# Two rounds of routed experts: setup of the routing tables rearranged in `experts`

## The chip, the cores and the metric

The kernel runs on one core of a Trainium2 chip. The metric is the device time in microseconds of one execution; the figure of a version is the median of its runs. Engines are named as in the profile: PE is TensorE, DVE is VectorE, ACT is ScalarE, POOL is GpSimd, and SP is the engine whose queue issues most transfers.

## The reference

The input has 4096 tokens of 256 features. Four layers are added to it one after the other; the change touches the two that route tokens to experts.

```python
# layer 1: eight experts, two per token, chosen from the context
logits = einsum('bsd,de->bse', context, Wg) + bg
scores, idx = top_k(logits, 2);  weights = softmax(scores)
combine = sum(one_hot(idx, E) * weights[..., None], axis=-2)
h = relu(einsum('bsd,edf->bsef', layernorm(x), W1) + b1)
x = x + einsum('bsed,bse->bsd', einsum('bsef,efd->bsed', h, W2) + b2, combine)
# layer 2: eight experts, one per token, chosen from the normalised x,
# at most tokens / 8 per expert, gate value softmax(logits) of the chosen one
...
# layer 3: attention with 16 heads; layer 4: gated FFN with fake quantisation
```

## The kernel before

`two_layers` calls `experts` twice, then `attention` and `gated_ffn`. In the first call (`choices` 2, `gate_source` the context, `capacity` None, 40 tiles of 256 slots) each token goes to two experts; in the second (`choices` 1, no gate source, a fixed capacity, 16 tiles) to one. The names of both calls' tiles begin with top_ in the trace, since it drops digits.

Each call has a setup and a loop over expert tiles. In the setup, the token rows (x_all, 32 tiles of 128 rows, loaded in four quarters) are measured for the layer norm on DVE (L649 to L654); ACT takes the root (L587 in the first call, behind the last `logits_copy`; L577 in the second), and DVE refines it and makes the scale and shift. PE transposes the gate source in groups of four tiles, multiplies by the gate weights and transposes the logits back (L424, L433, L440), with ACT copying in between (`gate_copy`, `logits_copy`). DVE then makes the choices: best logit, one-hot mask, lowest index, and PE counts how many tokens of each expert come before a token (L454, L455). From this DVE works out the slot of each token, as tile number and lane. The inverse, which token sits in a slot, comes from matrix products: for each choice DVE writes the masks pick_lane (128 x 4096, f16) and pick_tile (128 x 2560 in the first call, 128 x 1024 in the second), and PE multiplies them, 32 matmuls per choice (L461). From the product DVE makes row_of_slot, the row numbers for the gathers (L780 to L784). Before it waits for the product it writes expert_of_tile, which names the expert of a tile (L772 to L776).

Meanwhile ACT normalises x_all in place (L582; in the second call DVE does it, L668), and SP stores the result and the weights of each token by expert (by_token, eight columns in the same rows) to the DRAM tensor normed. `softmax_of_two` makes these weights on DVE between the picks of the two choices. POOL gathers rows of normed by row_of_slot (`gather`, L348), 128 rows at a time and two gathers to a tile. Six tiles are gathered ahead. Then, per tile, PE transposes the rows (L476), ACT and DVE split them into two f16 parts, PE does the first layer (L493 to L495), ACT the bias and the relu (L615), DVE splits (L805, L807), PE does the second layer (L511 to L513), DVE adds b2 and scales (`result`), and POOL adds the rows to x_sum in DRAM by an indirect transfer. Expert weights are loaded by SP into four buffers (`load_expert`), 512 KB each; ACT writes the high f16 part (`split_hi`) and DVE the low one (`split_lo`, L638), which also frees the buffer for the next expert's load. Expert 0 is split in the setup, the others one at a time before the tiles 1 to 7.

The order on each engine is the order in the code. `order(...)` makes the engine wait until the instruction has written; `order.tick` only counts it. SP's queue is, in order: gate weights and biases, context (first call), x, the copy of x to x_sum (first call), b2, expert 0, then a wait on s_normed, the normalised rows (4 MB in one transfer and two of 128 KB), a wait on s_wts, the token weights (128 KB in pieces of 32 bytes, and two of 4 KB), and then, in a loop, experts 1 to 7. POOL waits for the row table, s_stored and s_wstored ahead of its first gather. [...]

## Time and profile before

| what | value |
|---|---|
| median of three runs | 1664.61 us (1660.75 to 1664.78) |
| profiled execution | 1662.72 us, its span 1661.0 us |
| busy share of the span | PE 79%, PEld 64%, DVE 72%, ACT 50%, POOL 29% |
| first call, setup to the first expert product | 0 to 98.9 us |
| first call, expert tiles | 98.9 to about 546 us |
| second call, setup | about 553.6 to 626.2 us |
| PE busy, granted clock 0 to 60 us | 28.3 us, 0.86 |
| PE busy, granted clock 60 to 86 us | 4.6 us, 0.50 |
| DVE busy 60 to 86 us | 25.0 us |
| PE busy, granted clock 190 to 540 us | 349.1 us, 1.00 |

All times are microseconds from the start of the span. Busy time of an engine leaves out its waits and the issue of transfers. In the rows below, "L" with a number is the line of the kernel, "xN" the number of instructions that a row holds (its duration is from the start of the first to the end of the last), and square brackets give the idle time of the engine ahead of the row and what ended it. A buffer called top_w_hi or top_w_lo can be any of the small tiles that live in the unused parts of the weight buffers.

### The profile page before, as it was taken

The numbers are of one execution on the slowest core, as the hardware profiler recorded it, in microseconds if no ns is written. First come the engines' busy times: TensorE is split into PE (matmuls) and PEld (weight loads), VectorE is DVE, ScalarE is ACT, GpSimd is POOL, SyncE is SP. The second block draws the span as 40 slices with busy tenths as digits, with TensorE's granted clock in tenths as the row PEclk, the third lists the DMA queues.
The fourth block names the chain that finished last, engine by engine and source line by source line (L and its number), as shares of the span: only waits on it lengthen the run. The fifth ranks groups of instructions, "written<-read, shape, count | busy, mean of one in ns | idle before, by whom it ended". The sixth has DMA issues, their size and how long they took to land. (4 is left out here: it accounts for less than half of the span.)

```text
span 1661.0 us, 31750 instructions
## 1 busy us (share of the span) xinstructions
PE 1311.1 (79%) x10558; PEld 1068.2 (64%) x10559; DVE 1196.2 (72%) x2040; ACT 830.6 (50%) x1240; POOL 481.7 (29%) x480
## 2 busy tenths in 40 slices
PE   6069999999999529999368999999998499760087
PEld 3059888888898208998346887778877344320076
DVE  3869756655665478965178888888888576998854
ACT  3546533333333226733046555555555466987654
POOL 0035755555542114553212222222224000000000
PEclk9579999999999769999769888888888599995599
DMA  9548432233321656832430000000000100336211
GB/s 326 172 150 244 106 49 45 48 51 51 47 47 23 191 162 178 232 53 34 97 98 10 11 9 9 9 9 9 9 10 1 39 1 0 140 127 240 101 45 58
DMA packets 104166, 134.71 MB, mean 81 GB/s; under 512 B 16529, under 2 KB 88209, under 8 KB 102289
## 3 DMA queue, kind: packets, MB, share of 16 engines
q1 hardware_dynamic: 82576, 103.73, 19.1%
q0 software_dynamic: 21504, 29.83, 10.8%
q8 instruction: 55, 0.90, 0.2%
q14 instruction: 31, 0.25, 0.0%
HBM read 88.43 MB, written 45.11 MB: 80 GB/s over the span
## 5 line engine op out<-in xcount | busy, mean ns | idle before, releaser
L615 ACT ACTIVATE top_x_all<-top_h_ps,top_b1T 128x256 f32<-128x256 f32 x448 | 185.7, 472 | 311.6 <-PE top_h_ps L495 311.6
L493 PE MATMUL top_h_ps<-top_xT_hi,top_w_hi 128*128 128x256 f16 x896 | 246.3, 275 | 0.0
L494 PE MATMUL top_h_ps<-top_xT_lo,top_w_hi 128*128 128x256 f16 x896 | 246.2, 275 | 0.0
L495 PE MATMUL top_h_ps<-top_xT_hi,top_w_lo 128*128 128x256 f16 x896 | 246.1, 275 | 0.0
L513 PE MATMUL top_y_ps<-top_w_hi,top_x_all 128*128 x896 | 244.2, 273 | 0.0
L511 PE MATMUL top_y_ps<-top_w_hi,top_x_all 128*128 x896 | 244.2, 273 | 0.0
L512 PE MATMUL top_y_ps<-top_w_lo,top_x_all 128*128 x896 | 244.2, 273 | 0.0
L805 DVE CAST top_x_all<-top_x_all 128x512 f16<-128x512 f32 x224 | 98.5, 440 | 145.7 <-ACT top_x_all L615 145.7
L807 DVE TENSOR_TENSOR top_x_all<-top_x_all 128x512 f16<-128x512 f32 x224 | 155.7, 695 | 7.7
L353 POOL DMA_INDIRECT x_sum<-top_x_all,top_row_of_slot x56 | 101.5, 1812 | 173.3 <-DVE top_x_all L819 120.0
L1129 PEld LDWEIGHTS attn_out_ps<-attn_v,attn_probT 128*128 128x128 f32 x1024 | 127.1, 199 | 4.4
L1615 PE MATMUL ffn_ps<-ffn_dT_hi,ffn_yT 128*128 128x256 f16 x192 | 53.8, 280 | 91.1 <-DVE ffn_yT L1895 91.1
L1129 PE MATMUL attn_out_ps<-attn_v,attn_probT 128*128 128x17 f32 x1024 | 125.4, 265 | 0.0
L1028 POOL TENSOR_TENSOR attn_q_parts<-attn_q,attn_q_parts 128x512 f16<-128x512 f32 x32 | 37.1, 1158 | 303.9 <-ACT attn_q_parts L1192 303.9
L1119 PE MATMUL attn_S<-attn_ident,attn_prob 128*128 128x128 f32 x512 | 94.2, 344 | 38.9 <-ACT attn_prob L1208 38.8
L353 POOL DMA_INDIRECT x_sum<-top_x_all,top_rows_out x56 | 91.6, 1636 | 109.7 <-DVE top_x_all L819 98.5
L1212 ACT ACTIVATE attn_probT<-attn_S 128x1024 f32<-128x1024 f32 x64 | 65.5, 1023 | 89.9 <-PE attn_S L1119 89.9
L1327 DVE COPY_PREDICATED attn_S<-attn_masked,attn_tiny 128x1024 f32<-128x1024 int32 x64 | 104.4, 1632 | 1.3 <-PE attn_S L1113 1.3
L1119 PEld LDWEIGHTS attn_S<-attn_ident,attn_prob 128*128 128x128 f32 x512 | 74.0, 174 | 48.1 <-ACT attn_prob L1208 44.9
L348 POOL DMA_INDIRECT top_xg<-normed,top_row_of_slot x56 | 60.0, 1072 | 149.9 <-DVE top_row_of_slot L784 133.3
L1583 PE MATMUL ffn_ps<-ffn_yT,ffn_guT_hi 128*128 128x512 f16 x192 | 74.0, 385 | 27.5 <-ACT ffn_u_all L1656 23.3
L494 PEld LDWEIGHTS top_h_ps<-top_xT_lo,top_w_hi 128*128 x896 | 88.4, 99 | 10.9
(299 smaller groups left out, 3219.4 us busy)
## 6 DMA issues: line engine op xcount, KB each, us to landing
top_staged<-in_L_xattn_W SPq DMA_DIRECT2D x32, 512.0 KB, 6.2
top_staged<-in_L_ffn_w SPq DMA_DIRECT2D x32, 512.0 KB, 5.4
up_raw<-ffn_u_all SPq DMA_DIRECT2D x48, 256.0 KB, 2.1
ffn_yT<-up_raw SPq DMA_DIRECT2D x12, 1024.0 KB, 4.7
normed<-top_x_all SPq DMA_DIRECT2D x2, 4096.0 KB, 14.1
top_w_lo<-in_ctx SPq DMA_DIRECT2D x4, 1024.0 KB, 9.9
top_x_all<-in_x SPq DMA_DIRECT2D x4, 1024.0 KB, 11.8
x_sum<-top_x_all SPq DMA_DIRECT2D x4, 1024.0 KB, 11.6
```

The source lines that it names most:

```text
L353: nc.gpsimd.indirect_dma_start(out=x_sum, out_offset=bass.IndirectOffsetOnAxis(ap=rows, axis=0), in_=y[p][:, k, :], in_offset=None, comput ...
L493: nc.tensor.matmul(out, hi, xT_hi[p][:, c, :], start=(c == 0), stop=False)
L494: nc.tensor.matmul(out, hi, xT_lo[p][:, c, :], start=False, stop=False)
L495: last = nc.tensor.matmul(out, lo, xT_hi[p][:, c, :], start=False, stop=(c == DC - 1))
L511: nc.tensor.matmul(out, h_hi[p][:, fc, rows], hi, start=(fc == 0 and k == 0), stop=False, skip_group_check=True)
L512: nc.tensor.matmul(out, h_hi[p][:, fc, rows], lo, start=False, stop=False, skip_group_check=True)
L513: last = nc.tensor.matmul(out, h_lo[p][:, fc, rows], hi, start=False, stop=(fc == FC - 1), skip_group_check=True)
L615: last = nc.scalar.activation(h32[:, fc * R:(fc + 1) * R], h_ps[:, b, q * R:(q + 1) * R], ACT.Relu, bias=b1T[:, bass.ds(e * FC + fc, 1)], ...
L807: V.tensor_tensor(lo, part, hi, ALU.subtract).then_inc(s_hl[p], 1)
L1119: mm = nc.tensor.transpose(S[:, r, c, :], prob[:, r * HC + c, :], ident[:])
L1129: mm = nc.tensor.matmul(out_ps[:, h * V1:(h + 1) * V1], probT[:, h, :], v32[i][:, 2 * c + r, :], start=True, stop=True)
L1327: V.copy_predicated(S[:, r], masked[:].unsqueeze(1).to_broadcast(wide), tiny[:].unsqueeze(1).to_broadcast(wide)).then_inc(s_mask[r][p], 1)
```

## The change

The same values are computed.

- In the first call ACT takes the root ahead of the last `logits_copy`, not behind it. The normalised rows are written to the context's buffer (n_all), not in place. The wait for the copy of x to x_sum moves behind the normalisation and the split of expert 0.
- The rows are normalised and stored in quarters, each with its own wait on SP; POOL waits for 96 on s_stored.
- The load of b2 moves on SP's queue from ahead of expert 0 to behind the stores of the token weights. DVE waits for it ahead of `split_lo(0)`, not ahead of the logits.
- Three pairs of DVE instructions in the routing of the first call, one in that of the second, become one `scalar_tensor_tensor` each.
- The three products and sums that make by_token in the first call move from DVE to POOL, ahead of its gathers.
- Each choice writes pick_tile first and pick_lane in four quarters, and PE starts its matmuls quarter by quarter.
- The expert table is written behind the row table, with a semaphore of its own (s_experts), for which PE and ACT wait.

```diff
+        n_all = gate_all
...
-            sp.dma_start(b2_all[:].rearrange("p e d -> p (e d)"), broadcast_rows(b2, P, E * D)).then_inc(s_b2, 16)
...
             load_expert(0)
-            sp.wait_ge(s_normed, 1)
-            sp.dma_start(n_tiles, x_all[:]).then_inc(s_stored, 16)
+            for q in range(4):
+                sp.wait_ge(s_normed, q + 1)
+                sp.dma_start(n_tiles[:, q * n:(q + 1) * n, :], n_all[:, q * n:(q + 1) * n, :]).then_inc(s_stored, 16)
...
+            sp.dma_start(b2_all[:].rearrange("p e d -> p (e d)"), broadcast_rows(b2, P, E * D)).then_inc(s_b2, 16)
             with sp.Fori(1, E) as e:
                 load_expert(e)
...
+            if choices == 2:
+                pool.wait_ge(s_share, 1)
+                order.tick(nc.gpsimd.tensor_tensor(by_token[:], onehot[0], weight[0][:].unsqueeze(2).to_broadcast([P, T, E]), ALU.mult))
+                order(nc.gpsimd.tensor_tensor(both, onehot[1], weight[1][:].unsqueeze(2).to_broadcast([P, T, E]), ALU.mult))
+                nc.gpsimd.tensor_tensor(by_token[:], by_token[:], both, ALU.add).then_inc(s_wts, 1)
             pool.wait_ge(s_table, 1)
-            pool.wait_ge(s_stored, 48)
+            pool.wait_ge(s_stored, 96)
...
-                pe.wait_ge(s_pick, c + 1)
                 for t in range(T):
+                    if t % (T // 4) == 0:
+                        pe.wait_ge(s_pick, 4 * c + t // (T // 4) + 1)
...
             transpose_in(0, 0)
+            pe.wait_ge(s_experts, 1)
...
-            logits_copy(GROUPS - 1)
             if gate_source is not None:
                 act.wait_ge(s_var, 1)
                 nc.scalar.activation(rstd[:], rtmp[:], ACT.Sqrt).then_inc(s_root, 1)
+            logits_copy(GROUPS - 1)
...
-            dve.wait_ge(s_b2, 16)
             dve.wait_ge(s_lt, GROUPS)
...
-                order(V.tensor_scalar(work, work, float(E), None, ALU.mult))
-                order(V.tensor_tensor(work, work, of_expert(expert_no[:]), ALU.add))
+                order(V.scalar_tensor_tensor(work, work, float(E), of_expert(expert_no[:]), ALU.mult, ALU.add))
...
-                    order(V.tensor_scalar(work, onehot[c], -3e38, None, ALU.mult))
-                    order(V.tensor_tensor(logits, logits, work, ALU.add))
+                    order(V.scalar_tensor_tensor(logits, onehot[c], -3e38, logits, ALU.mult, ALU.add))
...
-                order.tick(V.tensor_tensor(pick_lane[c], lanes(P), by_lane(slot_mod[c][:], P), ALU.is_equal))
                 order(V.tensor_tensor(pick_tile[c], lanes(NS), by_lane(slot_div[c][:], NS), ALU.is_equal))
-                V.tensor_tensor(pick_tile[c], pick_tile[c], by_lane(token_v[:], NS), ALU.mult).then_inc(s_pick, 1)
+                V.tensor_tensor(pick_tile[c], pick_tile[c], by_lane(token_v[:], NS), ALU.mult)
+                for q in range(4):
+                    part = slice(q * (T // 4), (q + 1) * (T // 4))
+                    V.tensor_tensor(pick_lane[c][:, part], lanes(P)[:, part], by_lane(slot_mod[c][:], P)[:, part],
+                                    ALU.is_equal).then_inc(s_pick, 1)
...
             V.tensor_copy(row_of_slot[:], row_f[:]).then_inc(s_table, 1)
+            order(V.tensor_scalar(expert_f[:], lane_no[:, 0:NT], start_of[:, 1:2], None, ALU.is_ge))
+            for e in range(2, E):
+                order(V.scalar_tensor_tensor(expert_f[:], lane_no[:, 0:NT], start_of[:, e:e + 1], expert_f[:],
+                                             ALU.is_ge, ALU.add))
+            V.tensor_copy(expert_of_tile[:], expert_f[:]).then_inc(s_experts, 1)
             dve.wait_ge(s_table, 1)
+            dve.wait_ge(s_experts, 1)
+            dve.wait_ge(s_b2, 16)
             split_lo(dve, 0)
```

## Rows read from the trace of the kernel before

**Rows 1.** Timeline of the first call, last logits to the routing: start, duration, engine, line.

```profile
38.99 0.59 ACT L569 ACTIVATE top_w_lo<-top_xT_ps 8x512 f32<-8x512 f32 x1 [2.31 <-PE top_xT_ps L433]
39.59 1.28 ACT L587 ACT_TABLE_LOAD   x1
39.63 0.41 PE L440 MATMUL top_y_ps<-top_ident,top_w_lo 8*128 8x8 f32 x4 [0.68 <-ACT top_w_lo L569]
...
41.15 0.35 DVE L656 RECIPROCAL top_rstd<-top_rstd 128x32 f32<-128x32 f32 x1 [6.29 <-ACT top_rstd L587]
...
44.73 0.42 DVE L685 TENSOR_TENSOR top_w_hi<-top_y_ps,top_bg_sb 128x256 f32<-128x256 f32 x1 [2.10 <-DMA top_b_all<-in_L_xattn_b]
...
46.10 0.29 DVE L696 TENSOR_SCALAR top_w_hi<-top_w_hi 128x256 f32<-128x256 f32 x1
```

**Rows 2.** Timeline of the first call, picks, shares, expert table, reading of the product.

```profile
60.02 4.42 DVE L768 TENSOR_TENSOR top_w_hi<-top_lane_no,top_slot_mod 128x4096 f16<-128x4096 f32 x1
...
69.96 0.17 DVE L758 TENSOR_SCALAR top_weight<-top_weight 128x32 f32<-128x32 f32 x1
...
70.78 0.42 DVE L761 TENSOR_TENSOR top_by_token<-top_w_hi,top_weight 128x256 f32<-128x256 f32 x1
...
82.11 2.31 PE L461 MATMUL top_h_ps<-top_w_hi 128*128 128x80 f16 x32 [9.70 <-DVE top_w_hi L770]
82.24 1.74 DVE L774 SCALAR_TENSOR_TENSOR top_expert_f<-top_lane_no,top_start_of,top_expert_f 128x40 f32<-128x40 f32 x6
...
84.53 0.24 DVE L780 TENSOR_SCALAR top_pad_f<-top_h_ps 128x80 f32<-128x80 f32 x1 [0.34 <-PE top_h_ps L461]
```

**Rows 3.** Timeline of the first call from the row table on; then line L348's summary.

```profile
85.87 4.63 DVE L638 SCALAR_TENSOR_TENSOR top_w_lo<-top_staged,top_w_hi 128x1024 f16<-128x1024 f32 x4
...
88.57 1.64 POOL L348 DMA_INDIRECT top_xg<-normed,top_row_of_slot  x1 [0.30 <-issue]
...
95.83 1.11 PE L476 MATMUL top_xT_ps<-top_ident,top_xg 128*128 128x128 f32 x4 [11.41 <-DMA top_xg<-normed,top_row_of_slot]
...
98.94 0.42 PE L493 MATMUL top_h_ps<-top_xT_hi,top_w_hi 128*128 128x256 f16 x1
...
L348 POOL DMA_INDIRECT top_xg<-normed,top_row_of_slot x56: 942/1017/2113, 86.2 to 751.6; - x56
...
DMA to landing us min/median/max: 2.7/2.9/7.2
```

**Rows 4.** SP's queue: store of the token weights, its landings; b2's issues, KB, landing.

```profile
74.11 1.24 SPq L310 DMA_DIRECT2D normed<-top_by_token  x1
75.39 4.73 SPq L312 DMA_DIRECT2D normed<-top_by_token  x2
...
DMA to landing us min/median/max: 2.7/6.7/7.7
...
top_b_all<-in_L_xattn_b SPq DMA_DIRECT2D x1, 1024.0 KB, 7.8
top_b_all<-in_L_ffn_b SPq DMA_DIRECT2D x1, 1024.0 KB, 12.9
```

**Rows 5.** Timeline: GpSimd and VectorE instructions that run at the same time.

```profile
165.70 1.29 POOL L369 COPY top_rows_out<-top_row_of_slot 128x1 int32 x1 [3.42 <-DMA x_sum<-top_x_all,top_row_of_slot]
...
842.18 0.72 POOL L1025 TENSOR_TENSOR x_held<-x_held,attn_biases 128x256 f32<-128x256 f32 x1 [24.07 <-DVE attn_xn L1294]
...
859.73 1.60 DVE L1327 COPY_PREDICATED attn_S<-attn_masked,attn_tiny 128x1024 f32<-128x1024 int32 x1
```

**Rows 6.** Timeline of the second call: last x quarter, row table, gather, first tile.

```profile
571.03 2.71 DVE L649 BATCH_NORM_STATS2 top_stats<-top_x_all 128x6 f32<-128x256 f32 x8 [1.77 <-DMA top_x_all<-x_sum]
...
612.44 0.19 DVE L780 TENSOR_SCALAR top_pad_f<-top_h_ps 128x32 f32<-128x32 f32 x1
...
615.99 1.90 POOL L348 DMA_INDIRECT top_xg<-normed,top_row_of_slot  x1 [0.30 <-issue]
...
622.71 1.11 PE L476 MATMUL top_xT_ps<-top_ident,top_xg 128*128 128x128 f32 x4 [11.19 <-DMA top_xg<-normed,top_row_of_slot]
```

More of the change, by code:

```diff
@@ L211, in experts @@
         oh16 = sb("oh16", [P, T, E], F16)
+        both = routing(2).rearrange("p (t e) -> p t e", e=E)
         best = [sb(f"best{c}", [P, T], F32) for c in range(choices)]
@@ L250, in experts @@
         s_pick = sem("picks_ready"); s_picked = sem("picks_used")
-        s_table = sem("tables_ready")
+        s_table = sem("rows_ready"); s_experts = sem("experts_ready"); s_share = sem("weight_shares")
         s_rows = sem("row_columns_copied")
@@ L577, in _ @@
                     nc.scalar.activation(rstd[:], rtmp[:], ACT.Sqrt).then_inc(s_root, 1)
-            logits_copy(GROUPS - 1)
-            def normalise(first_tile, end):
-                for t in range(first_tile, end):
-                    mm = nc.scalar.activation(x_all[:, t, :], x_all[:, t, :], ACT.Identity, bias=shift[:, t:t + 1], scale=rstd[:, t:t + 1])
-                return mm
             if gate_source is not None:
@@ L587, in _, with normalise @@
                 nc.scalar.activation(rstd[:], rtmp[:], ACT.Sqrt).then_inc(s_root, 1)
+            logits_copy(GROUPS - 1)
+            def normalise(q):
+                for t in range(q * (T // 4), (q + 1) * (T // 4)):
+                    mm = nc.scalar.activation(n_all[:, t, :], x_all[:, t, :], ACT.Identity, bias=shift[:, t:t + 1], scale=rstd[:, t:t + 1])
+                mm.then_inc(s_normed, 1)
+            if gate_source is not None:
                 act.wait_ge(s_scales, 1)
-                act.wait_ge(s_begun, 96)
-                normalise(0, T // 4)
+                normalise(0)
             else:
@@ L595, in _ @@
                 nc.scalar.activation(weight[1][:], rtmp[:], ACT.Exp).then_inc(s_exp, 1)
-                normalise(T // 4, T).then_inc(s_normed, 1)
+                for q in range(1, 4):
+                    normalise(q)
                 split_hi(act, 0)
@@ L599, in _ @@
                 nc.scalar.activation(work, work, ACT.Exp).then_inc(s_exp, 1)
+            if gate_source is not None:
+                act.wait_ge(s_begun, 96)
             def x_high(m, p):
@@ L617, in hidden @@
                     last.then_inc(s_h32[p], 1)
-            act.wait_ge(s_table, 1)
+            act.wait_ge(s_experts, 1)
             x_high(0, 0)
@@ L667, in _ @@
                         dve.wait_ge(s_tr, t // GC + 1)
-                    order.tick(V.tensor_scalar(x_all[:, t, :], x_all[:, t, :], mean_var[:, t, 0:1], rstd[:, t:t + 1],
-                                               ALU.subtract, ALU.mult))
-                order.wait()
-                V.nop().then_inc(s_normed, 1)
+                    mm = V.tensor_scalar(x_all[:, t, :], x_all[:, t, :], mean_var[:, t, 0:1], rstd[:, t:t + 1],
+                                         ALU.subtract, ALU.mult)
+                    if (t + 1) % (T // 4) == 0:
+                        mm.then_inc(s_normed, 1)
             def by_expert(ap):
@@ L753, in lanes, with shares_of_two @@
                 return lane_no[:, 0:n].unsqueeze(1).to_broadcast([P, T, n])
-            def softmax_of_two():
+            def shares_of_two():
                 dve.wait_ge(s_exp, 1)
@@ L759, in softmax_of_two @@
                 order(V.reciprocal(weight[0][:], weight[0][:]))
-                order(V.tensor_tensor(weight[1][:], weight[1][:], weight[0][:], ALU.mult))
-                order(V.tensor_tensor(by_token[:], onehot[0], by_expert(weight[0][:]), ALU.mult))
-                order(V.tensor_tensor(work, onehot[1], by_expert(weight[1][:]), ALU.mult))
-                V.tensor_tensor(by_token[:], by_token[:], work, ALU.add).then_inc(s_wts, 1)
+                V.tensor_tensor(weight[1][:], weight[1][:], weight[0][:], ALU.mult).then_inc(s_share, 1)
             for c in range(choices):
                 if c == 1:
-                    softmax_of_two()
-                order.tick(V.tensor_tensor(pick_lane[c], lanes(P), by_lane(slot_mod[c][:], P), ALU.is_equal))
+                    shares_of_two()
                 order(V.tensor_tensor(pick_tile[c], lanes(NS), by_lane(slot_div[c][:], NS), ALU.is_equal))
-                V.tensor_tensor(pick_tile[c], pick_tile[c], by_lane(token_v[:], NS), ALU.mult).then_inc(s_pick, 1)
-            order(V.tensor_scalar(expert_f[:], lane_no[:, 0:NT], start_of[:, 1:2], None, ALU.is_ge))
-            for e in range(2, E):
-                order(V.scalar_tensor_tensor(expert_f[:], lane_no[:, 0:NT], start_of[:, e:e + 1], expert_f[:],
-                                             ALU.is_ge, ALU.add))
-            order(V.tensor_copy(expert_of_tile[:], expert_f[:]))
+                V.tensor_tensor(pick_tile[c], pick_tile[c], by_lane(token_v[:], NS), ALU.mult)
[3 more added lines that the diff above has]
+                                    ALU.is_equal).then_inc(s_pick, 1)
             dve.wait_ge(s_picked, 1)
```

2 lines of the change are left out of this document (1 added, 1 removed).

## The prediction, blind

> **What bounds the kernel now.** I read first where the experts function is not yet multiplying. It is called twice (top-2, then top-1 routing; the trace drops digits, so both show as top_), and in each call the expert tiles begin only when the routing is done; every microsecond saved ahead of the first expert product moves all that follows. The timeline of the first call gives the chain. The last logits are back at 40.04 us (39.63 + 0.41), but ScalarE loads a table (1.28 us) for the root only behind its last logits copy, VectorE waits for that root until 41.15, and then, at 42.63, waits another 2.10 us for b2, which no routing step reads [rows 1]. So the logits are added at 44.73. From there to the row table VectorE has no wait of note and is the bound: picks from 60.02, the last product of 32 matmuls at 82.11 to 84.42, row table complete just before the split begins at 85.87 [rows 2, 3]. Then GpSimd gathers, the second gather has landed at 95.83, and the first expert product starts at 98.94 [rows 3]. The second call has the same shape: table products read at 612.44, tile 0 transposed from 622.71 [rows 6].
>
> **Call 1, to the picks.** The root moves ahead of the last logits copy: ScalarE is free at 36.68 (38.99 less the 2.31 that it waits) [rows 1], so load and root end by 38.2, and the 1.48 us of VectorE work that lay between root (41.15) and shift (42.63) ends by 39.8 [rows 1]. The copy it was moved ahead of waits for its product until 38.99 in any case, so it costs nothing; the cover is 0.8 us. With b2 not awaited, the logits add starts at the last logits, 40.1: 4.6 us earlier. What is late next is the logits chain of TensorE and ScalarE, untouched. Three pairs of instructions become one each: 0.29 plus a gap of 0.04 us is saved per pair [rows 1], 1.0 in all. The two-input form is not there at 256 elements; its bounds are the 0.42 of the kind of L685 and, were it slower by its removed part, no gain, so 0 to 1.0; I take 1.0. Picks start at 60.02 - 5.6 = 54.4. The normalisation writes to another buffer in quarters and ends near 58.5; its stores leave from 44 on and are down long before the gathers.
>
> **Call 1, picks.** The first choice's picks take 9.94 us (60.02 to 69.96), 4.34 of them the lane pick (4.42, and the next starts 0.08 before its end), which leaves 5.60 for comparing and multiplying the tile pick [rows 2]; the lane pick becomes four of 1024 elements, by the split's four instructions of 1024 elements 4.63 us in all against 4.42 [rows 2, 3]. So 10.2 per choice, plus 0.82 for the three share instructions (69.96 to 70.78): last quarter ready at 54.4 + 10.2 + 0.8 + 10.2 = 75.6. TensorE then has 8 matmuls left, not 32: 24 x 0.066 us ((2.31 - 0.27)/31, the last one's 0.27 kept) off the 2.49 us from the last pick (82.04, just before the first matmul at 82.11) to the reading (84.53) leaves 0.9. With 1.3 for the row table (84.53 to 85.84, just before 85.87) it is ready at 77.8 [rows 2, 3]. The expert table (2.2 us: six of 1.74 in all, a first of about 0.25 and a cast of about 0.2) hid those 24 matmuls before; it now stands behind the row table, where the gathers cover it.
>
> **Call 1, the three products moved to GpSimd.** They run under VectorE's picks, and the rows speak against that. GpSimd's column copy took 1.29 us while VectorE ran the split (two SBUF inputs, 4.63 for four, about 1.15 each), though it copies one column, and VectorE's COPY_PREDICATED took 1.60 with a GpSimd product just in front, a little over the 1.2 of a VectorE instruction of 1024 elements [rows 3, 5]. A pick compares or multiplies two SBUF inputs as well. An addition of this size takes 0.72 us [rows 5]. Alone, three need 2.5 us: shares at 65.4, weights at 67.9. Taking turns with picks of 2.8, 2.8 and 1.15 us, as the rows show, the first waits 2.8, the second 2.8, the third 1.15 (6.75), each is run (3 x 0.7, in which VectorE waits): weights at about 65.4 + 8.9 = 74.3, row table at 77.8 + 2.1 = 79.9. I take the turns; both ends stay in the range.
> The Trainium skill (SBUF — State Buffer, "SBUF: two separate sides") says that the shared port pair is held for a whole instruction and the other engine fully blocks, for a VectorE instruction with two SBUF inputs against a GpSimd one that reads SBUF. By that rule the row table comes at 79.9, without it at 77.8; the trace agrees with it (the 1.29 us copy).
>
> **Call 1, stores and biases behind the weights.** The weights store and two small ones go to SP's queue once the weights are there. Before, they took 8.3 us from 74.11 to the last landing (issued until 80.12, landings 2.7 to 7.7), with the 4 MB of rows still ahead on the queue [rows 4]. Now the queue is empty: below by the issue without back-pressure and one landing, 1.2 + 0.8 + 2.7 = 4.7; above 8.3; I take 6.5, so 74.3 + 6.5 = 80.8, 0.9 later than the row table, and gathers start at 81.1 (79.4 to 82.9). Before they started at 86.15. The first two took 2.11 and 1.64 us with the split beside them; the least for one is 0.94 [rows 3]. Now they meet the small expert-table instructions, so the second is issued at about 82.4. Its landing took 7.2 us with 2 MB of expert 1 behind it; the median of gathers is 2.9 [rows 3]. Expert 1 now starts after the gathers but b2 is in flight: I take 4.5, transposes at 86.9, product at 86.9 + 3.1 = 90.0.
> b2 is issued last, when the stores' issue is over (about 5 us after the weights: 79.3). It landed in 7.8 us in call 1 and 12.9 in call 2, with x and an expert's weights on the queue around it each time [rows 4]; with only the gathers beside it I take 6.6, an estimate a little under the lower: b2 at 85.9. VectorE waits there with the split of expert 0 (4.63) and the first x_low (0.85) behind it, and TensorE's first product behind those: 85.9 + 5.6 = 91.5. This is the later of the two and sets the start: 98.94 - 91.5 = **7.4 us** gained. Bounds: no turns and quick stores, 85.6 (13.3 us); b2 landing as in call 2 (12.9) with its issue a microsecond later, 93.2 + 5.6 = 98.8 (0.1 us).
>
> **Call 2.** The root stays where it is; the weights stay on VectorE. One fused pair gives 0.3. The lane pick in quarters costs 0.2. The expert table (2.1 us by the instructions of call 1) stood whole between last pick and reading, since the matmuls are shorter here; eight matmuls and a wait, 0.7, take its place: 1.4 less. So the row table is 1.5 us earlier. Behind it the second gather no longer meets the whole split and is issued at 613.8, not 615.99 [rows 6], ahead of expert 1's loads; landing 3.9 (2.9 to 6.7 as before): transposes at 617.7 against 622.71, **5.0 us** (2.2 to 6). VectorE is at 614.1 + 4.63 = 618.8 with the split, before x_low is due at 619.5, so the later expert table costs nothing; b2, issued near 602.5, lands by 615.4 even with 12.9 us. At the front b2 no longer follows the x quarters; the last quarter came 1.77 us after VectorE was ready for it, the others 0.3 [rows 6]. If b2's traffic was the cause it saves 1.5, if expert 0's (which now takes its place) nothing: 0.7.
>
> **Sum.** 7.4 + 5.0 + 0.7 = 13.1 us. The profiled execution took 1662.72 us (span 1661.0 and 1.7 around it): 1649.6. It lies 1.9 us under the median of the runs, 1664.61, so I predict 1651.5.
>
> **Rivals.**
> (a) b2 and turns as above, total gain 9 to 17 us: 0.5.
> (b) GpSimd is not held up: the row table at 77.8, b2 early, call 1 gains 12 to 13, total 18 to 20, about 1645. For it: GpSimd may take its three products in one turn; against: rows 5. 0.15.
> (c) The stores and b2 are as slow as in the loaded rows: gathers at 82.9, b2 at 92, first product at 97.6, call 1 gains 1.3, total 5 to 9, about 1657.5. For it: 4096 pieces of 32 bytes went slowly before. Against: rows no longer lie ahead. 0.22.
> (d) The change does not do what it says: the earlier start is eaten in the first eight tiles, which are paced by the expert loads and splits. Then 1662 to 1665. Against: these loads are released by the splits, which move along. 0.09.
> (e) Slower: the b2 wait. Each microsecond that b2 lands after 93.3 in call 1 costs one, and it turns the whole only past 93.3 + 5.7 = 99, a landing of 20 us, at over 1664.6; the slowest b2 row is 12.9. 0.04.
>
> **Range and chances.** (a) and (b) reach down to 1645; (c) up to 1659: 1645 to 1659, leaving out (d), (e) and a tail. A change under 0.3% (5 us) is about what a measurement of this kernel can't tell from none. (a), (b) and most of (c) are beyond it: faster 0.87; (d) and the rest of (c) within it: 0.09; slower 0.04.
>
> **What would show it.** The add of L685's kind starts near 40.1 without a wait; three GpSimd TENSOR_TENSORs of over 1.5 us on average, and picks with gaps or lengthened by 0.7; row table near 79.9; VectorE idle before the split with b2 as releaser, ending near 86; the first gathers near 1 us each; first expert product near 91.5, and in call 2 near 620.5 less what call 1 gained. If VectorE does not wait for b2, (b) or a gather-bound start holds; if the b2 wait ends past 90, (c). The forecast is wrong if the distance from first product to end grows.

## The result, and the profile after

The changed kernel took **1652.49 us** (median of 5 runs, 1651.43 to 1660.80) against 1664.61 before: ratio 0.9945, 95% interval 0.9929 to 0.9961, faster by 9 us (6 to 12) by the ratio and by 12.1 by the medians. I had predicted 1651.5. The number came out, but in part by luck: call 1 gained what I forecast by another path, call 2 gained a third of its forecast, and some of the rest was chance.

The profiled execution is the one of 1660.80, the slowest of the five. Its first two calls are 11.1 us shorter than before, while the attention stage, whose code is untouched, took 499.2 us against 489.9. The windows over that stage show why. Each row has the stretch, its length, the busy time of PE with its number of instructions, the granted clock, the DMA share and the GB/s. Before:

```profile
1000.00:1200.00 200.00, 184.19 (x1536) 0.88 0.03 10
1200.00:1300.00 100.00, 90.44 (x706) 0.82 0.02 5
```

After:

```profile
1000.00:1200.00 200.00, 184.83 (x1518) 0.85 0.03 9
1200.00:1300.00 100.00, 89.72 (x644) 0.75 0.02 5
```

The busy time is the same and the clock was granted for less of it, so fewer instructions got done. In the twelve profiled executions of variants below the stage took 489.0 to 493.6 us. So I compare the two calls by stages, and leave this stage aside.

**Front of call 1** (timeline after, all engines; [rows 1] before):

```profile
35.76 1.28 ACT L589 ACT_TABLE_LOAD   x1
...
38.05 0.59 ACT L578 ACTIVATE top_w_lo<-top_xT_ps 8x512 f32<-8x512 f32 x1 [0.77 <-PE top_xT_ps L440]
39.22 0.42 DVE L696 TENSOR_TENSOR top_w_hi<-top_y_ps,top_bg_sb 128x256 f32<-128x256 f32 x1 [0.43 <-PE top_y_ps L447]
...
40.59 0.42 DVE L707 SCALAR_TENSOR_TENSOR top_w_hi<-top_w_hi,top_expert_no 128x256 f32<-128x256 f32 x1
41.05 0.42 DVE L708 TENSOR_REDUCE top_first<-top_w_hi 128x32 f32<-128x256 f32 x1
```

The table load lies in the gap, the last logits copy still waits for PE (0.77), and the add waits for the logits alone. It starts 5.5 us earlier. Of that, 0.9 is the logits' own product, which came at 38.69 us for 39.63 before though nothing in its chain was changed; in the variants with this front the add started anywhere from 39.0 to 40.7 us. The fused instruction costs 0.42 and starts 0.46 before the next.

**Picks, shares, row table** ([rows 2] before):

```profile
59.11 4.62 DVE L778 TENSOR_TENSOR top_w_hi<-top_lane_no,top_slot_mod 128x1024 f16<-128x1024 f32 x4
...
64.35 2.82 DVE L774 TENSOR_TENSOR top_w_hi<-top_lane_no,top_slot_div 128x2560 f16<-128x2560 f32 x1
64.52 3.13 POOL L386 TENSOR_TENSOR top_by_token<-top_w_hi,top_weight 128x256 f32<-128x256 f32 x1 [54.01 <-DVE top_weight L769]
67.20 3.13 DVE L775 TENSOR_TENSOR top_w_hi<-top_w_hi,top_token_v 128x2560 f16<-128x2560 f16 x1
67.62 3.20 POOL L387 TENSOR_TENSOR top_w_hi<-top_w_hi,top_weight 128x256 f32<-128x256 f32 x1
70.26 5.58 DVE L778 TENSOR_TENSOR top_w_hi<-top_lane_no,top_slot_mod 128x1024 f16<-128x1024 f32 x4
70.90 1.58 POOL L388 TENSOR_TENSOR top_by_token<-top_by_token,top_w_hi 128x256 f32<-128x256 f32 x1
...
75.89 0.71 PE L469 MATMUL top_h_ps<-top_w_hi 128*128 128x80 f16 x8 [0.42 <-DVE top_w_hi L778]
76.65 0.24 DVE L784 TENSOR_SCALAR top_pad_f<-top_h_ps 128x80 f32<-128x80 f32 x1 [0.81 <-PE top_h_ps L469]
```

GpSimd and VectorE take turns: GpSimd's first two products last about as long as VectorE's picks beside them, and the picks of the second choice are longer than those of the first by 0.31 (3.13 against 2.82) and 0.96 us (5.58 against 4.62). Eight matmuls are left behind the last pick. The row table is ready at 77.95.

**From the row table to the first product** ([rows 3, 4] before; SP's queue, GpSimd, VectorE, PE):

```profile
72.92 2.54 SPq L313 DMA_DIRECT2D normed<-top_by_token  x2
75.50 0.43 SPq L314 DMA_DIRECT2D top_b_all<-in_L_xattn_b  x1
78.30 1.29 POOL L350 DMA_INDIRECT top_xg<-normed,top_row_of_slot  x1 [5.82 <-DVE top_row_of_slot L788]
79.90 0.96 POOL L350 DMA_INDIRECT top_xg<-normed,top_row_of_slot  x1 [0.30 <-issue]
80.89 4.63 DVE L650 SCALAR_TENSOR_TENSOR top_w_lo<-top_staged,top_w_hi 128x1024 f16<-128x1024 f32 x4 [0.78 <-DMA top_b_all<-in_L_xattn_b]
81.16 1.77 POOL L350 DMA_INDIRECT top_xg<-normed,top_row_of_slot  x1 [0.30 <-issue]
82.29 1.46 SPq L297 DMA_DIRECT2D top_staged<-in_L_xattn_W  x2
82.79 1.12 PE L484 MATMUL top_xT_ps<-top_ident,top_xg 128*128 128x128 f32 x4 [6.18 <-DMA top_xg<-normed,top_row_of_slot]
83.24 1.96 POOL L350 DMA_INDIRECT top_xg<-normed,top_row_of_slot  x1 [0.31 <-issue]
85.51 0.68 DVE L805 TENSOR_TENSOR top_xT_lo<-top_xT_ps,top_xT_hi 128x512 f16<-128x512 f32 x1
90.43 1.11 PE L484 MATMUL top_xT_ps<-top_ident,top_xg 128*128 128x128 f32 x4 [6.53 <-DMA top_xg<-normed,top_row_of_slot]
91.33 0.42 PE L501 MATMUL top_h_ps<-top_xT_hi,top_w_hi 128*128 128x256 f16 x1
```

This is the group to read slowly. The stores hold nothing up (the first gather is released by the row table), and b2 holds VectorE for 0.78 us, ahead of the split of expert 0. Tile 0 is transposed at 82.79 and its low part is there at 86.2. But the first product stands at 91.33, directly behind a second set of transposes, which waited until 90.43 for a gather: those of **tile 1**. `tiles` issues `transpose_in(q, i + 1)` ahead of the products of tile i, and PE's queue is in order. Before, the same second set stood at 98.03, 2.2 us behind the first, and tile 0's own low part was there only at 98.54, so the set hid there:

```profile
97.86 0.68 DVE L794 TENSOR_TENSOR top_xT_lo<-top_xT_ps,top_xT_hi 128x512 f16<-128x512 f32 x1
98.03 1.11 PE L476 MATMUL top_xT_ps<-top_ident,top_xg 128*128 128x128 f32 x4 [1.09 <-DMA top_xg<-normed,top_row_of_slot]
```

**Call 2** ([rows 6] before; VectorE, then PE):

```profile
559.36 2.71 DVE L661 BATCH_NORM_STATS2 top_stats<-top_x_all 128x6 f32<-128x256 f32 x8 [1.65 <-DMA top_x_all<-x_sum]
562.36 2.71 DVE L661 BATCH_NORM_STATS2 top_stats<-top_x_all 128x6 f32<-128x256 f32 x8 [0.28 <-DMA top_x_all<-x_sum]
...
607.63 1.11 PE L484 MATMUL top_xT_ps<-top_ident,top_xg 128*128 128x128 f32 x4 [5.59 <-DMA top_xg<-normed,top_row_of_slot]
614.85 1.12 PE L484 MATMUL top_xT_ps<-top_ident,top_xg 128*128 128x128 f32 x4 [6.10 <-DMA top_xg<-normed,top_row_of_slot]
```

It begins at 545.02 (its first issue), 553.56 before. Counted from there tile 0 is transposed at 62.61 (69.15 before), tile 1 at 69.83 (71.72), and the first product starts at 70.73 (72.63). The late quarter of x is now the third (1.65) instead of the fourth (1.77).

The stages of all the profiled executions, read from their timelines (us; "rest" is from the first product to the start of the next stage; the ratio is to the kernel before in the same session):

```
                 call 1          call 2           ratio to before, 95% interval
                 product  rest   product  rest
before            98.94  454.62   72.63  190.42
after             91.33  453.69   70.73  189.72   0.9945 (0.9929 to 0.9961)
loads_held        87.58  456.28   67.15  194.00   0.9948 (0.9932 to 0.9965)
tile0_first       87.57  460.39   65.71  198.59   0.9968 (0.9957 to 0.9979)
both              87.75  458.26   65.82  197.33   0.9939 (0.9922 to 0.9955)
weights_on_dve    91.22  453.85   70.87  189.92   0.9927 (0.9911 to 0.9944)
table_first       94.31  453.64   72.79  192.99   0.9969 (0.9956 to 0.9982)
front_only        93.89  453.29   72.16  190.56   0.9961 (0.9947 to 0.9975)
whole_picks       94.73  454.23   70.89  189.89   0.9970 (0.9957 to 0.9982)
b2_early          91.19  453.06   70.57  192.09   0.9947 (0.9930 to 0.9964)
split_late        92.79  453.16   71.26  190.69   0.9929 (0.9907 to 0.9951)
loads_later       89.53  455.93   67.28  195.12   0.9940 (0.9915 to 0.9965)
tile1_mid         86.65  453.67   66.00  193.06   0.9891 (0.9869 to 0.9913)
before_mid        98.58  454.04   72.02  191.12   0.9995 (0.9985 to 1.0004)
```

From before to after: 7.61 + 0.93 in call 1, 1.90 + 0.70 in call 2, 11.1 us.

Each row is one execution, so small differences of the rest need care. All the kernels settle at 10.9 us per tile behind the first eight tiles, and what they differ by arises within those eight. There chance has a part: b2_early has the first product of call 2 where the changed kernel has it (70.57), and yet a rest that is 2.4 us longer.

### The profile page after: what moved, and what is told of

The parts are those of the page before. It is cut to its first block and busy times, and to the rows that moved or that the text cites. A ratio compares the mean times of both kernels' runs of the same rounds, so it can differ in the third digit from the quotient of the medians.

```text
span 1659.0 us, 31759 instructions
## 1 busy us (share of the span) xinstructions
PE 1325.0 (80%) x10558; PEld 1081.1 (65%) x10559; DVE 1193.9 (72%) x2042; ACT 833.8 (50%) x1240; POOL 483.5 (29%) x483
## 5 line engine op out<-in xcount | busy, mean ns | idle before, releaser
L816 DVE CAST top_x_all<-top_x_all 128x512 f16<-128x512 f32 x224 | 98.5, 440 | 145.1 <-ACT top_x_all L627 145.1
L355 POOL DMA_INDIRECT x_sum<-top_x_all,top_row_of_slot x56 | 94.6, 1690 | 177.4 <-DVE top_x_all L830 163.0
L1140 PEld LDWEIGHTS attn_out_ps<-attn_v,attn_probT 128*128 128x128 f32 x1024 | 138.6, 214 | 4.7 <-issue 0.3
L1140 PE MATMUL attn_out_ps<-attn_v,attn_probT 128*128 128x17 f32 x1024 | 135.9, 276 | 0.0
L1130 PE MATMUL attn_S<-attn_ident,attn_prob 128*128 128x128 f32 x512 | 83.3, 315 | 36.0 <-ACT attn_prob L1219 35.9
L503 PEld LDWEIGHTS top_h_ps<-top_xT_hi,top_w_lo 128*128 x896 | 88.3, 98 | 10.7
L501 PEld LDWEIGHTS top_h_ps<-top_xT_hi,top_w_hi 128*128 x896 | 88.3, 99 | 10.0
```

What stands on the lines that cost most here:

```text
L355: nc.gpsimd.indirect_dma_start(out=x_sum, out_offset=bass.IndirectOffsetOnAxis(ap=rows, axis=0), in_=y[p][:, k, :], in_offset=None, comput ...
L501: nc.tensor.matmul(out, hi, xT_hi[p][:, c, :], start=(c == 0), stop=False)
L503: last = nc.tensor.matmul(out, lo, xT_hi[p][:, c, :], start=False, stop=(c == DC - 1))
L816: V.tensor_copy(hi, part).then_inc(s_hh[p], 1)
L1140: mm = nc.tensor.matmul(out_ps[:, h * V1:(h + 1) * V1], probT[:, h, :], v32[i][:, 2 * c + r, :], start=True, stop=True)
```

## The experiments

The theories: **A**, the first product waits for tile 1's gather because of the order in PE's queue, and expert 1's loads (2 MB) slow that gather; **B**, what slows it is GpSimd's issue of the gather meeting VectorE's split; **C**, the first eight tiles are paced by loads and splits of the experts, so the start is worth little. All but front_only and before_mid are edits of the changed kernel.

**loads_held.** Expert 1's loads wait for tile 1's gathers.

```diff
+            sp.wait_ge(s_xg[1], 32)
             with sp.Fori(1, E) as e:
                 load_expert(e)
```

> Changed kernel, but SP waits for both gathers of tile 1 (s_xg[1] at 32) before it issues expert 1. Theory A: after the change the first expert product waits for tile 1's gather, because PE has tile 1's transposes ahead of tile 0's products, and that gather is slow (9.2 and 7.2 us from issue) because 2 MB of expert 1 are on the DMA engines: then tile 1's transposes come near 87 in call 1, not 90.4, the first product near 87.9, not 91.3, and about 3.5 us per call are gained, 7 us in all (about 1645.5). Theory B: the gather is slow because its issue on GpSimd meets the split of expert 0 (1.77 and 1.96 us for 0.95), not because of the loads: then at most 1 us per call is gained. Theory C: the start of the products does not matter, the first eight tiles are paced by the expert loads: no gain or a loss of 1 to 4 us, since expert 1 arrives 5 us later.

The timeline of loads_held:

```profile
82.92 1.96 POOL L351 DMA_INDIRECT top_xg<-normed,top_row_of_slot  x1 [0.30 <-issue]
86.67 1.11 PE L485 MATMUL top_xT_ps<-top_ident,top_xg 128*128 128x128 f32 x4 [3.06 <-DMA top_xg<-normed,top_row_of_slot]
...
90.93 0.84 ACT L628 ACTIVATE top_x_all<-top_h_ps,top_b1T 128x256 f32<-128x256 f32 x2 [2.51 <-PE top_h_ps L504]
96.74 2.30 ACT L628 ACTIVATE top_x_all<-top_h_ps,top_b1T 128x256 f32<-128x256 f32 x6 [4.97 <-PE top_h_ps L504]
...
96.52 0.49 PE L485 MATMUL top_xT_ps<-top_ident,top_xg 128*128 128x128 f32 x3 [1.07 <-issue]
```

The issue beside the split still takes 1.96 us, and yet tile 1's transposes start 3.8 us earlier (3.5 counted from the logits add): A, not B, for the landing. The first products come 3.7 and 3.6 us earlier. But ScalarE then stands 4.97 us (5.01 in call 2) before its second eviction (the relu of the second quarter of tile 0's hidden layer), whose input had been there since about 92.5, and the rest of the calls grows by 2.6 and 4.3 us. The ratio is that of the changed kernel, not the 7 us less that A gave: something gives the gain back, as C says.

**tile0_first.** Tile 1's transposes and parts wholly behind tile 0's first layer.

```diff
-                    if more or i + 1 < AHEAD:
+                    early = first_tile and i == 0
+                    if (more or i + 1 < AHEAD) and not early:
                         transpose_in(q, i + 1)
...
                             layer2(m - 1 + p, 1 - p, e_before, fc)
+                    if early:
+                        transpose_in(q, i + 1)
```

On ScalarE and VectorE the high and low part of tile 1 move behind tile 0's hidden layer in the same way.

> Changed kernel, but for tile 0 alone PE does the first layer before the transposes of tile 1, and ScalarE and VectorE handle tile 0's hidden part before tile 1's x part; loads as they are. Theory A: the first product starts when tile 0's low part is there, near 86.3 in call 1 (5 us earlier), and as tile 1 is used only behind it, 2 to 4 us per call reach the end. Theory C: the first product starts 5 us earlier and the end of the call does not move (under 1 us). If the first product does not start earlier, the wait was not PE's queue order.

**both** holds the loads as well.

> Changed kernel with both edits, expert 1's loads held back until tile 1 is gathered and tile 0's products ahead of tile 1's transposes. Theory A: the first product starts near 86.3 in call 1 and tile 1 is in by 87, so 4 to 5 us per call, 8 to 10 in all (about 1643). If the gains of the two edits are the same gain, it is no better than the better of them.

In tile0_first the first products came at 87.57 and 65.71, 5.0 us earlier in each call (in call 1 counted from the logits add), as forecast; the rest grew by 6.7 and 8.9 us, where A had 2 to 4 us per call reach the end. The median is 1659.50 us, slower than the changed kernel. The timeline of tile0_first, call 1:

```profile
96.86 0.61 ACT L620 ACTIVATE top_xT_hi<-top_xT_ps 128x512 f16<-128x512 f32 x1
98.65 0.68 DVE L811 TENSOR_TENSOR top_xT_lo<-top_xT_ps,top_xT_hi 128x512 f16<-128x512 f32 x1
99.54 0.39 PE L501 MATMUL top_h_ps<-top_xT_hi,top_w_hi 128*128 128x256 f16 x1 [3.75 <-issue]
```

PE stands 3.75 us between tile 0 and tile 1 for tile 1's parts, which used to be made under tile 0's products. From the last product of tile 0 to the first of tile 1 it is 4.9 us, 0.5 in the changed kernel; what is left of the 6.7 goes in the tiles behind. One wait was traded for another, and the run says nothing yet against the start being worth its time. With both edits the loss is 4.6 and 7.6 us, and the median 1654.32 for the 1643 that A gave.

**weights_on_dve.** The three products of the token weights go back to VectorE, nothing else.

```diff
+                order(V.tensor_tensor(by_token[:], onehot[0], by_expert(weight[0][:]), ALU.mult))
+                order(V.tensor_tensor(work, onehot[1], by_expert(weight[1][:]), ALU.mult))
+                V.tensor_tensor(by_token[:], by_token[:], work, ALU.add).then_inc(s_wts, 1)
...
-                pool.wait_ge(s_share, 1)
```

> Changed kernel, but the three products that make the token weights are back on VectorE, as before the change. Turn-taking theory: VectorE pays 1.3 us for them but no longer gets its picks lengthened (3.13 for 2.82 and 5.58 for 4.62 in the changed kernel), so the row table moves by less than 0.3 us, while the weights are ready near 65.7, not 72.5; the total stays within 0.1%. Offload theory: the row table comes 1.3 us later and so does the end (about 0.08%).

The row table came 38.86 us behind the logits add, against 38.73; first products and rest are the same within 0.2 us, the ratio is 0.9927, its interval overlaps that of the changed kernel. The turn-taking theory holds, and moving the products gained nothing that can be told. What VectorE no longer does it loses in turns: 3 x 0.46 us, by the spacing of such instructions above, against 0.31 + 0.96.

**table_first.** The expert table goes back ahead of the reading of the product.

> Changed kernel, but the expert table is written ahead of the row table, as before the change. My sum: row table 1.3 us later in call 1 (2.2 less the 0.9 that the last matmuls and the wait take) and 1.4 us in call 2; gathers then meet the split of expert 0 and the loads of expert 1 sooner after their issue, which costs another 1 to 3 us on the first gather but, if tile 1's gather sets the start, only its share in that: first product 1.5 to 3 us later per call, 3 to 6 us in all. Rival: since the split of expert 0 and so the loads of expert 1 start at the same time in either order, tile 1's gather lands at nearly the same time and the loss is under 1 us per call.

Row table 1.3 and 1.4 us later; first products 3.0 us later in call 1 (2.0 when counted from the logits add) and 2.1 in call 2, as my sum had it; ratio 0.9969. The order of the two tables is worth 2 us in each call at the first product. The rest of call 2 grew by 3.3 as well, but b2_early's grew by 2.4 with the start where it was, so that is not shown to come from the order.

**front_only.** The kernel before with two edits: root ahead of the last logits copy, b2 loaded behind the weights' stores and awaited ahead of the split.

> Kernel before with two edits alone: the root ahead of the last logits copy, and b2 loaded behind the token weights and awaited ahead of the split of expert 0. My sum says that the logits are added at 40.1, not 44.73, so the row table and the first product come 4.6 us earlier in call 1 and call 2 stays as it is (0 to 1.5 us from the x quarters): about 1660. Rival: the store of the 4 MB of normalised rows, issued when ScalarE has normalised them all, and the weights store behind it are now late, since ScalarE's normalisation moves by less than VectorE's chain; then GpSimd waits for the stores and the gain is 1 to 3 us.

First product 5.05 us earlier in call 1, 0.5 in call 2; ratio 0.9961. Two small moves give 6.7 of the 11.1 us, 5.5 of them ahead of the first products and 1.2 behind (my sum had 4.6 and up to 1.5 from the x quarters).

**whole_picks.** The four lane picks become one instruction again.

> Changed kernel, but each lane pick is one instruction of 4096 elements again, still behind the tile pick. My sum: VectorE saves 0.2 us per choice and PE needs 24 more matmuls behind the last pick (1.6 us in call 1, 0.8 in call 2): row table 1.2 us later in call 1, 0.6 in call 2, first products the same, about 1.8 us in all (0.1%). Rival: with fewer instruction ends GpSimd's third product waits a whole lane pick (4.4 us), weights and b2 come 3 us later and set the start: 3 us or more in call 1.

The timeline of whole_picks:

```profile
71.05 4.79 POOL L388 TENSOR_TENSOR top_by_token<-top_by_token,top_w_hi 128x256 f32<-128x256 f32 x1
...
81.71 1.29 POOL L350 DMA_INDIRECT top_xg<-normed,top_row_of_slot  x1 [5.87 <-DMA normed<-top_by_token]
```

GpSimd's third product waits out a pick of 4096 elements (4.79 us, 1.58 with quarters), so the weights are ready at 75.84, and now the stores release the first gather, 2.7 us behind the row table (78.97). Weights to gather take 5.9 us. In call 2, where GpSimd has no products, the first product moved by 0.16. Counted from the logits add the row table is 0.7 us later, the matmuls' part, and the first product 3.0. So the quarters are worth 3 us in call 1, most of it through the other engine's turn: the rival, not my sum.

**b2_early.** b2 is loaded ahead of expert 0 again; the wait stays ahead of the split.

> Changed kernel, but b2 is loaded where it was, ahead of expert 0; it is still awaited only ahead of the split of expert 0. If b2's place on the queue did nothing of its own, the time is the same within 0.1%: VectorE's wait of 0.8 us for b2 in call 1 goes and the split of expert 0 and expert 1's loads start 0.8 us earlier, which costs or gains under 1 us at tile 1's gather. If its traffic beside the first gathers slowed them, tile 0 is in 1 us earlier; if its traffic beside x in call 2 mattered, the last x quarter comes 1.5 us later and so does the end.

First products within 0.2 us, ratio 0.9947: b2's place on the queue is worth nothing that shows at the first products once nobody waits for it. The x quarter in call 2 is late as before (1.66 us).

**split_late.** VectorE's split of expert 0 waits for a count that GpSimd gives behind its fourth gather.

```diff
+            dve.wait_ge(s_issued, 1)
             split_lo(dve, 0)
...
+                if j == 1:
+                    pool.sem_inc(s_issued)
```

> VectorE starts the low halves of expert 0 only when GpSimd has issued the four gathers of the first two tiles. Theory I (the issue is what delays tile 1's gather: the third and fourth issue took 1.77 and 1.96 us with the split beside them, against 0.95 alone): the four issues end at about 83.2 instead of 85.2, tile 1's rows land near 88.4 instead of 90.4, the low half of tile 0's columns comes at about 88.8, and the first product at about 89.2 instead of 91.3, 2 us earlier in each call. Theory L (the landing is what delays it, because expert 1's loads, 2 MB, move at the same time): the issues shorten as said, but the loads are released by the split and so also start about 2.3 us later, so the landing may shorten by more than the issue: first product near 88.9, bound by the split; if expert 1's loads set it, the gap from the fourth issue's end to the transposes, 5.2 us now, falls toward the 3.0 that the first gathers took. For the whole, theory C (what follows the start eats it, as with the held loads) gives a median within 2 us of the changed kernel; otherwise 3 to 5 us less.

It tells nothing apart: the split started at 82.47, released by b2, ahead of the third gather's 82.62, and the issues took 1.89 and 1.97 us. GpSimd gave the count before its gathers were issued. The issue's share in the delay stays unmeasured.

**loads_later.** Expert 1's loads wait for tile 0's second eviction (`sp.wait_ge(s_h32[0], 2)` ahead of the loop).

> Expert 1's loads are held until ScalarE has evicted the second quarter of tile 0's hidden layer, near 90 us after a first product at 87.6. With the loads held only until tile 1's rows had landed, ScalarE stood 4.97 us before its second eviction, with its input long ready. Theory Q (the stall is a fetch of instructions, which are run here for the first time, queued behind the 2 MB of expert 1's loads): with the loads out of the way the stall is gone, the four evictions follow each other at the pace of the changed kernel (2.2, 1.3 and 1.3 us apart), and the second product block of tile 0 ends at about 95; the price is that expert 1's halves come 3 to 4 us later, which the queue of ScalarE shows as a wait for DMA before the split. Theory E (the stall belongs to something that runs on ScalarE or TensorE at that place, not to the loads): a gap of 4 us or more stays before the second eviction although no load is moving. The median: between 1648 and 1655 if the start's gain of 3.7 us in each call survives, 1655 to 1660 if the later loads cost more than they free.

The timeline of loads_later (ScalarE):

```profile
92.26 0.84 ACT L628 ACTIVATE top_x_all<-top_h_ps,top_b1T 128x256 f32<-128x256 f32 x2 [1.89 <-PE top_h_ps L504]
93.55 0.84 ACT L628 ACTIVATE top_x_all<-top_h_ps,top_b1T 128x256 f32<-128x256 f32 x2 [0.45 <-PE top_h_ps L504]
...
99.10 1.06 ACT L559 ACTIVATE top_w_hi<-top_staged 128x1024 f16<-128x1024 f32 x1 [2.09 <-DMA top_staged<-in_L_xattn_W]
100.74 1.06 ACT L559 ACTIVATE top_w_hi<-top_staged 128x1024 f16<-128x1024 f32 x1 [0.58 <-DMA top_staged<-in_L_xattn_W]
```

The stall is gone (evictions 1.29 us apart, as the products come) and a wait for the loads has taken its place: ScalarE runs the split of expert 1 in its queue ahead of tile 2's high part, so a load that is late is late for everybody. The rest is 2.2 and 5.4 us longer. So between these two runs the stall comes and goes with loads that move beside tile 0 (in loads_held they ran from 87.0 to about 96.5 us, and the stall ended at 96.74), and holding the loads, at either of these two points, gives the start's gain back. But moving loads alone do not make it: in tile1_mid below they move until about 93 us, and its second eviction, at 91.06, waits 0.68 us. That the stalled engine waited for instructions to be fetched I could not show: in loads_held one packet of the instruction queue falls between 90 and 91 us, before the stall begins. Its cause stays open.

**tile1_mid.** Tile 1's transposes stand behind the fourth of tile 0's eight column blocks, its high and low parts behind the second eviction; the loads stay.

```diff
                         layer1(m, p, e, fc)
+                        if early and fc == 3:
+                            transpose_in(q, i + 1)
...
+                    if first and b == 1:
+                        x_high(m + p, 1 - p)
...
+                    if first and b == 2:
+                        x_low(0, 1)
```

> Tile 1's transposes stand in the middle of tile 0's first layer (behind the fourth of its eight column blocks), and tile 1's high and low parts behind the second quarter on ScalarE and VectorE; so tile 0's products wait for nothing but its own columns, and tile 1 is ready when they end. Theory A (the start is worth what it moves): first product at about 87.5 in call 1 and 65.7 in call 2, tile 1's transposes at 91.0 to 91.5, no gap of TensorE before tile 1's products; both calls 3 to 5 us shorter, median near 1645. Theory C (what comes behind the start is paced by instruction fetches and expert 1's loads): the first product is early as said, but gaps of ScalarE or TensorE of 2 to 5 us appear within tile 0, between the first and the third quarter, and the median stays between 1650 and 1656. Putting tile 1 wholly behind tile 0 had lost 6.7 and 8.9 us after the first product; if the loss here is as large, that was not the missing cover of tile 1's parts but the code path.

The timeline of tile1_mid (ScalarE, VectorE, PE):

```profile
89.55 0.84 ACT L630 ACTIVATE top_x_all<-top_h_ps,top_b1T 128x256 f32<-128x256 f32 x2 [4.48 <-PE top_h_ps L503]
91.06 0.84 ACT L630 ACTIVATE top_x_all<-top_h_ps,top_b1T 128x256 f32<-128x256 f32 x2 [0.68 <-PE top_h_ps L503]
91.79 0.60 ACT L620 ACTIVATE top_xT_hi<-top_xT_ps 128x512 f16<-128x512 f32 x1
...
93.30 0.68 DVE L811 TENSOR_TENSOR top_xT_lo<-top_xT_ps,top_xT_hi 128x512 f16<-128x512 f32 x1
...
86.65 0.39 PE L501 MATMUL top_h_ps<-top_xT_hi,top_w_hi 128*128 128x256 f16 x1 [2.31 <-DVE top_xT_lo L811]
90.89 0.66 PE L484 MATMUL top_xT_ps<-top_ident,top_xg 128*128 128x128 f32 x4
```

The first product waits for its own low part alone, and tile 1's transposes wait for nothing. Median **1645.55 us** (1644.56 to 1646.87), ratio 0.9891: 18 us by the ratio for the change's 9, and the fastest version here. In call 1 the 4.7 us of the start arrive at the end whole (rest 453.67 against 453.69; tile 0's products took as long as before, 7.3 us, since fewer of them at the lower clock made up for the transposes in their midst), so C falls there. In call 2 this execution keeps 1.4 of 4.7: 2.1 us go in tile 0 (first to last of its 48 products 8.3 us, 6.2 after), 1.2 in later tiles. Of the 2.1, 0.7 are tile 1's four transposes, which now stand between the products, and 1.4 more products at TensorE's lower clock (last section). As b2_early lost 2.4 us in this stage without the edit, the loss is not shown to be the edit's.

**before_mid.** The same edit on the kernel before.

> The kernel before, with nothing of the change, but with tile 1's transposes and parts in the middle of tile 0's first layer, the edit that made the changed kernel 7 us faster. Theory S (the two edits serve each other: before the change both first tiles' gathers landed within 2.2 us of each other, so there was hardly anything to win by not waiting for tile 1's): the low part of tile 0 ends at 98.54 in the profile of before and the first product stands at 98.94, in call 2 at 625.42 and 626.19, so the first products come 0.3 and 0.7 us earlier, the time falls by 0 to 2 us, ratio about 0.9995 to 1.000. Theory G (the order in TensorE's queue is worth its 7 us by itself, because it also takes other waits out of tile 0 and tile 1): the time falls by 5 us or more, ratio 0.997 or lower, and what the change is worth is 12 us in either order of the queue.

First products 0.36 and 0.61 us earlier, 1662.05 us against 1663.02, ratio 0.9995 with an interval that holds 1. The edit is worth nothing that can be told from noise before the change, and 7 to 9 us after it. (By medians 6.9; in ratios 0.0054 of 1663 us, though the changed kernel and tile1_mid were not run in the same session. Ahead of the first products it is 9.4.) It is the change's own gain, which had been stopped at tile 1.

## Why the prediction was right, and where it was not

- **The front of call 1** was right: 4.6 us at the logits add (5.5 less the 0.9 of the start), 1.0 us from the three fused pairs. front_only shows it by itself.
- **Picks.** Starting 0.9 us earlier than forecast, the last quarter was ready at 75.84 instead of 77.7. Turns were right in kind. Their cost to VectorE was mis-sized, 1.27 us for the 2.1 I took. The weights came 8.1 us behind the shares, forecast 8.9. The Trainium skill (SBUF — State Buffer, "SBUF: two separate sides") has the other engine blocked for a whole instruction; the 3.13, 3.20, 1.58 and 4.79 us of GpSimd, against 0.72 [rows 5], agree for GpSimd. VectorE's loss of 1.27 us is less than the 2.2 (3 x 0.72) that full blocking for three products would cost, so for VectorE the trace does not bear the rule out as a price.
- **Stores**: 5.9 us from the weights to the gather in whole_picks, where they release it; forecast 6.5. Right in size, but in the changed kernel they were not the later of the two, the row table was. The three issues took 3.0 us, for the 2.0 in my lower bound and the 5 that I took for b2.
- **b2** failed. I had it issued 5 us after the weights and landing in 6.6; it was issued after 3.0 and landed in 5.2, at 80.8 for the forecast 85.9. It cost 0.78 us, not the start. Rivals (c) and (e) hung on it and fell with it; (b) was nearer, with b2 early and the row table at 77.95 for its 77.8, but by luck: GpSimd was held up, and the early start and the cheaper turns made up for it. Its 12 to 13 us did not come either.
- **The step that failed** is "this is the later of the two and sets the start". There was a third: tile 1's gather. The 3.1 us that I took from transposes to product had it in them already (the second set at 98.03 above); I read them as tile 0's own path. In the changed kernel tile 0 was transposed at 82.8 for the 86.9 forecast, and that distance was 8.5 us, with tile 0's low part ready 5.1 us before the product. Call 1's first product, forecast at 91.5 by b2, came at 91.33 by the gather. Two errors met: b2 early by 5 us, a wait overlooked of 5 us.
- **Call 2** shows the same error without the luck: tile 0's transposes 6.5 us earlier (5.0 forecast), first product 1.9. Row table 1.8 earlier (1.5 forecast).
- **x quarters**: 0.1 us for 0.7. b2_early shows that b2's traffic was not the cause.
- **Behind the start** 1.6 us more were gained than I counted. Luck has a part: 1.0 of them lie in the 48 products of each tile 0, which took 7.3 and 6.2 us for 7.7 and 6.9 before, with fewer at the lower clock. The distance from first product to end did not grow, so rival (d) fell. For a start that is earlier still it holds in part, by another way than I argued: held loads give it back.
- **Sum**: 7.6 + 1.9 + 1.6 = 11.1 in the profiled calls, against 7.4 + 5.7 = 13.1; the medians gave 12.1.

Open: what the engines wait for in the stall of loads_held; how much of tile 1's late gather is its issue; where call 2 of tile1_mid loses its last 1.2 us, and b2_early its 2.4.

## What to carry to other kernels

Ahead of a first product list everything that stands before it in that engine's queue, the next tile's preparation too: a wait that was hidden behind a late start becomes the start when the front gets faster. Place such a prefetch in the middle of the work it is meant to hide under, not ahead of it (the first item waits) nor behind it (the second does). And read the duration that you reuse as a chain of waits, not as a cost.

## What the runs showed of the hardware

- Taking turns was one-sided here: GpSimd needed 7.9 us for three products beside VectorE's picks, and VectorE lost 1.27. With short instructions on VectorE GpSimd had its turn sooner (1.58 us beside picks of 1024 elements, 4.79 beside one of 4096).
- The issue of an indirect gather took 1.1 to 2.1 us where VectorE's two-input split ran beside the whole of it (1.10 the third issue of b2_early, 2.11 the first before the change), and 0.95 otherwise (the first of a series 1.0 to 1.3, a few later ones up to 1.2).
- 2 MB of plain loads that started beside a gather delayed its landing by 3.5 us (PE waited 6.53 us for it, 3.06 with the loads held).
- TensorE stood at the lower of its two clocks, 1.2 GHz, when the products began: in the changed kernel the granted clock was 0.50 from 60 to 82 us, with 5.7 us busy, and 0.50 from 91.0 to 95.5, with PE busy throughout; from 96.0 to 98.5 it was 1.00 (2.4 GHz). Over all the profiles it rose 2.3 to 5.9 us behind the first product, with 10 to 26 products at 0.21 us apart instead of 0.11, in no order that the edits explain: up to 1.7 us of jitter in each call. In tile1_mid's call 2 there were 23, in the changed kernel's 10: 1.4 of the 2.1 us lost there in tile 0.
